# Attention step: Q projected directly behind K, z and output in the score banks, scores last; two qv_out buffers, one pos_qv

## What is computed

```
def step(carry, qkv):                      # two segments of 64 rows, one after the other
    mem, zc = carry
    qs, ks, vs = qkv
    sq = elu(qs) + 1.0
    mem = mem + einsum('bhsk,bhsv->bhkv', sq, vs)
    zc = zc + (elu(ks) + 1.0).sum(axis=-2, keepdims=True)
    scores = einsum('bhsk,bhtk->bhst', qs, ks) * scale
    att_dot = einsum('bhst,bhtv->bhsv', softmax(scores, axis=-1), vs)
    num = einsum('bhsk,bhkv->bhsv', sq, mem)
    den = sq.sum(axis=-1, keepdims=True) * zc
    att = gate * (num / den) + (1.0 - gate) * att_dot
    return ((mem, zc), att.reshape(Bx, L, H * DV) @ Wo)
x = layernorm(x + attention(x))
```

## Time and profile before

| | |
|---|---|
| timed runs, median (lowest to highest) | 1029.44 us (1025.58 to 1029.86) |
| profiled execution, its own time | 1023.68 us |
| its span | 1021.9 us |
| granted TensorE clock, mean over the span | 0.851 |
| PE busy | 791.6 us, 77% |
| DVE, ACT, POOL busy | 619.2, 542.7, 515.4 us |

### The profile page before, as it was taken

The page is one execution under the profiler, slowest core; times in us unless marked ns, Lnnn a source line. Parts: engine busy times, 40 slices in busy tenths (PEclk is TensorE's granted clock), DMA queues, the critical chain, the costliest instruction groups (busy, mean ns, idle before and its releaser), DMA issues. The chain is left out here.

```text
span 1021.9 us, 26750 instructions
## 1 busy us (share of the span) xinstructions
PE 791.6 (77%) x9501; PEld 683.3 (67%) x9502; DVE 619.2 (61%) x1217; ACT 542.7 (53%) x1119; POOL 515.4 (50%) x524
## 2 busy tenths in 40 slices
PE   5688898899988899889989899987599450099940
PEld 4577777787877778778778787877366450089940
DVE  4466666666766767666676676766588450034438
ACT  4656666656676566665676666672222110067730
POOL 2364546655565555565555645564334116546742
PEclk8788989988998989898898988998799655589985
DMA  6565655655655665565655656654118501140023
GB/s 211 133 179 137 146 135 144 144 165 144 144 144 144 165 150 138 144 144 165 156 132 144 149 161 149 138 146 123 49 32 232 64 1 44 52 107 31 31 74 111
DMA packets 115499, 127.71 MB, mean 125 GB/s; under 512 B 6913, under 2 KB 101409, under 8 KB 109329
## 3 DMA queue, kind: packets, MB, share of 16 engines
q1 hardware_dynamic: 112928, 122.17, 48.1%
q0 software_dynamic: 2544, 5.21, 1.5%
HBM read 67.42 MB, written 43.16 MB: 108 GB/s over the span
## 5 line engine op out<-in xcount | busy, mean ns | idle before, releaser
L304 POOL TENSOR_TENSOR ps<-s_exp,row_rec 128x512 f32<-128x512 f32 x64 | 66.7, 1045 | 202.5 <-DVE row_rec L669 202.5
L326 POOL TENSOR_TENSOR lhs<-pos_qv,ungate 64x1024 f32<-64x1024 f32 x64 | 150.6, 2353 | 2.5
L313 POOL TENSOR_TENSOR e_qk<-e_qk 128x512 f32<-128x512 f32 (+2 forms) x96 | 79.3, 826 | 90.0 <-DVE e_qk L637 85.0
L502 ACT ACTIVATE s_exp<-s_exp 128x512 f32<-128x512 f32 x64 | 40.2, 628 | 137.0 <-DVE s_exp L717 137.0
L645 DVE SCALAR_TENSOR_TENSOR qv_out<-bank,e_qk 128x512 f32<-128x512 f32 x64 | 44.2, 692 | 104.4 <-ACT e_qk L526 103.5
L401 PE MATMUL bank<-const,ps 128*128 128x128 f32 x512 | 94.1, 342 | 2.9 <-issue 2.5
L657 DVE TENSOR_TENSOR lhs<-mix,zg_all 64x512 f32<-64x512 f32 x128 | 88.3, 690 | 7.5 <-DMA zg_all<-scratch_z 3.6
L579 ACT ACTIVATE psT<-bank 128x512 f32<-128x512 f32 x128 | 72.4, 595 | 22.1 <-PE bank L401 21.8
L427 PE MATMUL bank<-kT,qkT 64*64 64x64 f32 x2048 | 83.0, 249 | 0.0
L372 PE MATMUL bank<-w_v,x_cur 128*128 128x512 f32 x192 | 77.7, 559 | 3.6 <-DVE w_v L603 3.6
L401 PEld LDWEIGHTS bank<-const,ps 128*128 128x128 f32 x512 | 74.3, 175 | 8.7 <-issue 3.0
(11 more groups left out here) (210 smaller groups left out, 1684.8 us busy)
## 6 DMA issues: line engine op xcount, KB each, us to landing
scratch_qv<-qv_out SPq DMA_DIRECT2D x32, 1024.0 KB, 4.0
pos_qv<-scratch_qv SPq DMA_DIRECT2D x64, 512.0 KB, 6.2
kT<-qkT SPq DMA_DIRECT2D x32, 512.0 KB, 4.1
zg_all<-scratch_z SPq DMA_DIRECT2D x64, 256.0 KB, 3.8
sorted_x<-padding SPq DMA_DIRECT2D x1, 2515.5 KB, 20.7
r_all<-in_x_dram SPq DMA_DIRECT2D x4, 512.0 KB, 6.7
cx<-in_ctx_dram SPq DMA_DIRECT2D x8, 256.0 KB, 2.8
w<-in_L_ffn_W_dram SPq DMA_DIRECT2D x1, 2048.0 KB, 9.4
```

The lines of the kernel that those rows point to most:

```text
L313: pool.tensor_tensor(dst, e_qk[:, 0:c, DK:], e_qk[:, c:2 * c, DK:], ALU.add).then_inc(k_summed, 1)
L326: pool.tensor_tensor(lhs[0:L, 1 - n, :, :], pos_qv[q][s, :, DK:], ungate[s, :, :], ALU.mult).then_inc(vg_ready, 1)
```

## The change

It writes the lists of the engines in another order and moves buffers:

- PE: Q is projected directly behind V and K. The z sum goes into score_bank[0] and the output into score_bank[1], where they were in proj_bank. output follows remember and is now for t - 2, no longer t - 3. All four turn_ps follow output, and the scores stand last in the step, where they were between the second and third turn_ps; they wait for res_ready, since the output shares their bank.
- qv_out has two buffers, pos_qv one. So SP's reload of pos_qv waits for mem_ready and vg_ready of the step before.
- DVE: sq_sum and its reciprocal stand directly behind zg and ahead of cut_k; evac_memory(0) stands ahead of cut_q(0), evac_memory(1) ahead of cut_q(1); the residual follows cut_q(1); all evac_memory precede the row maxima.
- ACT: the first exponential is at the head of the next step, evac_att behind the copies of Q, all four psT copies together.
- POOL: ps<-pos_qv stands ahead of k_sum, and the copy to x_cur last.

```diff
@@ attention_phase
-        qv_out = sb("qv_out", [P, C, 2 * DK])
+        qv_out = [sb(f"qv_out{i}", [P, C, 2 * DK]) for i in range(2)]
-        pos_qv = [sb(f"pos_qv{i}", [P, H, 2 * DK]) for i in range(2)]
+        pos_qv = sb("pos_qv", [P, H, 2 * DK])
@@ SP step
                     sp.wait_ge(stored_qv, 16 * t)
+                    if not is_step(u, 0):
+                        sp.wait_ge(mem_ready, 2 * u)
+                        sp.wait_ge(vg_ready, 2 * u)
@@ PE turn_qk
-                        pe.wait_ge(shifted, 2 * t - 1 + f)
+                        pe.wait_ge(*((z_rec, t), (shifted, 2 * t))[f])
@@ PE step
                     pe.wait_ge(v_evac, t + 1)
+                    for hh in range(2):
+                        project(proj_bank, w_q, hh, q_proj)
                 if two:
...
+                    pe.wait_ge(shifted, 2 * t - 1)
                     pe.wait_ge(k_summed, 4 * t)
-                    pe.matmul(proj_bank[0][0:SEG * H, 0:DK], cst("z_sum"), k_sum[:, :], start=True, stop=True).then_inc(zc_ready, 1)
-                if four:
...
-                    output(t - 3)
+                    pe.matmul(score_bank[0][0:SEG * H, 0:DK], cst("z_sum"), k_sum[:, :], start=True, stop=True).then_inc(zc_ready, 1)
                 if three:
                     attend(t - 2, 0)
                     attend(t - 2, 1)
                 if one:
-                    if is_step(t, 0):
-                        pe.wait_ge(w_split, 6)
-                    if two:
-                        pe.wait_ge(z_rec, t)
-                    project(proj_bank, w_q, 0, q_proj)
-                    if four:
-                        pe.wait_ge(res_ready, t - 2)
-                    project(proj_bank, w_q, 1, q_proj)
                     for f in range(4):
                         turn_qk(f)
                 if two:
                     remember(0)
                     remember(1)
-                    turn_ps(0)
-                    turn_ps(1)
-                if one:
+                if three:
...
+                    output(t - 2)
+                if two:
+                    for f in range(4):
+                        turn_ps(f)
+                if one:
+                    if three:
+                        pe.wait_ge(res_ready, t - 1)
                     score(0)
                     score(1)
-                if two:
-                    turn_ps(2)
-                    turn_ps(3)
@@ DVE step
                     dve.tensor_tensor(zg[:, :], z[:, :], gate[:, :], ALU.mult).then_inc(z_ready, 1)
+                if two:
+
+                    dve.wait_ge(qv_loaded, 32 * t)
+                    if not is_step(u, 0):
+                        dve.wait_ge(sqn_ready, u)
+                    dve.tensor_reduce(sq_sum[:, :], pos_qv[:, :, 0:DK], X, ALU.add).then_inc(sq_summed, 1)
+                    dve.wait_ge(sq_summed, t)
+                    dve.reciprocal(sq_rec[:, :], sq_sum[:, :]).then_inc(sq_inv, 1)
                 if one:
                     cut_k(0)
-                if not is_step(t, 0, 1, 2):
-                    residual(t - 3)
-                if one:
                     cut_k(1)
                 if not is_step(t, 0, 1):
                     move_att(t - 2)
                 if two:
-
-                    dve.wait_ge(qv_loaded[q], 32 * (hq + 1))
...
+                    evac_memory(0)
                 if one:
                     cut_q(0)
                 if two:
-                    evac_memory(0)
+                    evac_memory(1)
                 if one:
                     cut_q(1)
-                if two:
-                    evac_memory(1)
+                if not is_step(t, 0, 1):
+                    residual(t - 2)
+                if two:
+                    evac_memory(2)
+                    evac_memory(3)
```

More of the change, by code:

```diff
@@ L211, in attention_phase @@
         stored_qv, stored_z, z_loaded = sem("stored_qv"), sem("stored_z"), sem("z_loaded")
-        qv_loaded = [sem(f"qv_loaded{i}") for i in range(2)]
+        qv_loaded = sem("qv_loaded")
         vg_ready = sem("vg_ready")
@@ L358, in output @@
                 for c in range(C // 2):
-                    last = pe.matmul(proj_bank[1][:, 0:D], attT[:, c, :], w_o[:, c, :], start=(c == 0), stop=(c == C // 2 - 1))
+                    last = pe.matmul(score_bank[1][:, 0:D], attT[:, c, :], w_o[:, c, :], start=(c == 0), stop=(c == C // 2 - 1))
                 last.then_inc(out_ready, 1)
@@ L413, in remember @@
                         odd, at = h % 2, (h // 2 % 4 * 2 + n) * DK
-                        last = pe.matmul(mix[odd * DK:(odd + 1) * DK, h // 8, at:at + DK], pos_qv[q][0:k, h, 0:DK],
-                                         pos_qv[q][0:k, h, DK:], start=True, stop=True)
+                        last = pe.matmul(mix[odd * DK:(odd + 1) * DK, h // 8, at:at + DK], pos_qv[0:k, h, 0:DK],
+                                         pos_qv[0:k, h, DK:], start=True, stop=True)
                     last.then_inc(mem_ready, 1)
@@ L531, in step @@
                         act.wait_ge(v_proj, 2 * t + hh + 1)
-                        if hh == 0 and not is_step(t, 0):
-                            act.wait_ge(stored_qv, 16 * t)
-                        last = act.activation(qv_out[:, c, DK:], src, ACT.Copy)
+                        if hh == 0 and not is_step(t, 0, 1):
+                            act.wait_ge(stored_qv, 16 * u)
+                        last = act.activation(qv_out[p][:, c, DK:], src, ACT.Copy)
                     last.then_inc(v_evac, 1)
@@ L561, in step @@
                         act.activation(qk_tok[:, c, 0:DK], src, ACT.Copy).then_inc(q_evac, 1)
+                if three:
+                    evac_att(t - 2)
+                if one:
                     for f in range(4):
@@ L642, in cut_q @@
                     dve.wait_ge(q_grown, 2 * t + hh + 1)
-                    if hh == 0 and not is_step(t, 0):
-                        dve.wait_ge(stored_qv, 16 * t)
-                    dve.scalar_tensor_tensor(qv_out[:, c, 0:DK], proj_bank[hh][:, :].rearrange("p (c k) -> p c k", c=8), 0.0,
+                    dve.scalar_tensor_tensor(qv_out[p][:, c, 0:DK], proj_bank[hh][:, :].rearrange("p (c k) -> p c k", c=8), 0.0,
                                              e_qk[:, c, 0:DK], ALU.max, ALU.add).then_inc(sq_ready, 1)
@@ L692, in step @@
                 if two:
-                    dve.wait_ge(qv_loaded[q], 32 * (hq + 1))
-                    if not is_step(u, 0):
-                        dve.wait_ge(sqn_ready, u)
-                    dve.tensor_reduce(sq_sum[:, :], pos_qv[q][:, :, 0:DK], X, ALU.add).then_inc(sq_summed, 1)
-                    dve.wait_ge(sq_summed, t)
-                    dve.reciprocal(sq_rec[:, :], sq_sum[:, :]).then_inc(sq_inv, 1)
+                    evac_memory(0)
                 if one:
@@ L718, in step @@
                                           ALU.subtract).then_inc(shifted, 1)
-                if two:
-                    evac_memory(2)
-                    evac_memory(3)
             run_steps(dve, step, B, peeled=2)
-            residual(B - 2)
             move_att(B - 1)
```

56 lines of the change are left out of this document (23 added, 33 removed).

## The result

The changed kernel takes 1071.63 us (median of 4 runs, 1070.77 to 1072.03), the kernel before 1027.51 us beside it; the ratio is 1.043, 95% interval 1.040 to 1.046. The forecast was 1074 us, the range 1038 to 1108. The profiled execution of the changed kernel had 1071.37 us and a span of 1069.5 us.

What follows compares the result with a forecast made beforehand. A loop through the pos_qv store and reload was taken to bound each step: 21.9 us, with 0.9 for half clock 22.8. 1023.7 + 48.4 - 1.5 = 1070.6, and 3.4 more gives 1074 us, range 1038 to 1108.

Steps and rivals of the forecast that it cites:

- The loop: Reload landing through sq_sum, cut_k, move_att, remember, evac_memory and cut_q to store and next reload: 21.9 us a step, no slack.
- The toll of the clock: Half clock on TensorE's remember, behind idle time: 0.9 us a step taken, between bounds of nothing and 2.15.
- The upper bound: Half clock meeting remember in each step, taking twice as long: 2.15 us a step.
- The kT wait: TensorE's wait for kT ahead of the scores goes: 62.4 us in 32 times, 1.82 us in the step shown.
- The single pos_qv does not bind: The reload's wait for the single buffer: lhs ends at landing + 11.4 us, the reload is issued at + 13.9.
- The drain: End of the attention phase: saves about 1.5 us, as one output of 2.0 us is gone from it.
- Profiled against timed: Timed runs lie 1.9 to 6.2 us above the profiled execution, median 5.8; 3.4 us added.
- A loop without any toll: Rival: the loop through the reload at 21.9 us a step with no half-clock cost, 1046 us; chance 0.2.
- remember at half clock in every step: Rival: remember on TensorE always at half clock, 24.05 us a step, 1113 us; chance 0.16.
- "Faster": Rival: loop shorter than counted, TensorE still bounds, 19.4 us a step, 970 us; chance 0.05 with what lies between.
- The rule on waits: Issue a DMA early, wait late: by it sq_sum's new place is a loss, VectorE standing still about 2 us.

Runs made afterwards that it cites:

- e7: The changed kernel with qv_out stored twice, first into a row of scratch_qv that nobody reads: 1164.79 us, ratio 1.135.
- e3: The changed kernel with both cut_q ahead of the first two evac_memory, sq_sum still early: 995.43 us, ratio 0.973.
- e2: The changed kernel with sq_sum and its reciprocal behind cut_k and move_att, and x_cur's copy at the head of POOL's list: 1011.79 us, ratio 0.988.
- e6: The changed kernel with each group of attend matmuls issued twice in a row: 1058.85 us, ratio 1.032.
- e11: The changed kernel with two buffers for pos_qv again, nothing else: 1068.51 us, ratio 1.043.
- e10: The changed kernel with both cut_q ahead of evac_memory and two buffers for pos_qv: 967.49 us, ratio 0.944.
- e5: The kernel before with sq_sum and its reciprocal directly behind zg, ahead of cut_k: 1056.53 us, ratio 1.028.
- e1: The changed kernel with sq_sum and its reciprocal put back behind cut_k and move_att: 1053.18 us, ratio 1.028.
- e4: The changed kernel with sq_sum behind move_att, x_cur first on POOL and cut_q ahead of evac_memory: 982.95 us, ratio 0.959.
- e9: The changed kernel with cut_q ahead of evac_memory and x_cur's copy at the head of POOL's list, sq_sum still early: 997.37 us, ratio 0.974.
- e8: The changed kernel with sq_sum behind move_att, x_cur first, cut_q ahead of evac_memory and two buffers for pos_qv: 932.20 us, ratio 0.910.

## Why the prediction was right

- **The loop.** Counted 21.9 us at full clock, measured 21.87 in the step shown and 21.7 on average of the ten at full clock, and all of its links are in the timeline in the order given. e7 shows that there is no slack in it, e3 that it breaks when cut_q leaves it, e2 that it breaks when sq_sum does and x_cur does not take its place. The parts were off a little and balance: landing to cut_q 9.5 us measured from sq_sum (9.6 counted), store and reload to sq_sum 12.4 (12.3 counted).
- **The toll of the clock.** 0.9 us a step taken, 22.67 - 21.87 = 0.80 measured, 1.0 on remember's own busy time. It was put on the right instruction, but the number was a choice between two bounds, and that it fits is in part luck. The upper bound was too high: half clock costs remember 3.88 - 2.23 = 1.65 us and not 2.15 (the rows that I leaned on, 3.68 against 2.08, give a factor of 1.8 and not 2). And two thirds of the steps pay 1.45 each (23.2 against 21.7), the others nothing, which nothing in the prediction could have told. The cause I gave, idle time ahead of remember, was tested by e6 and holds for about 0.5 of the 0.8, with the idle time ahead of the transposes.
- **The kT wait** went, as forecast (6.3 us left).
- **The single pos_qv does not bind**: right for this kernel (e11, 3 us), but the loop of 19.6 us that I passed over as slack bound as soon as cut_q was early (e10).
- **The drain.** This step of the sum failed: forecast -1.5 us, measured +3.2. I counted the output that falls away and not that TensorE, idle for 7.1 us there, would run remember, the output and the first transposes at half clock.
- **Profiled against timed.** I added 3.4 us for the difference of the two; the changed kernel's profiled execution is 0.3 under its median. That the total came within 2.4 us is in part luck: the steps (48.4 forecast, 44.1 measured) and this offset were too high by 4.3 and 3.1, the drain too low by 4.7, and the start of the phase, 0.9 longer, was not in the sum.
- **The rivals.** A loop without any toll (21.9 a step) and remember at half clock in every step (24.05) are both out at 22.67 as a rule for all steps, though the first describes a third of them, and the second, at 23.2 and not 24.05, two thirds. "Faster" was right in its condition: it decides when the chain from cut_q to the landing no longer holds TensorE. e3 did it by starting the chain earlier, not by shortening it, and came out 2.7% below the kernel before.
- **The rule on waits.** The rule of the Trainium skill, DMA: Bandwidth & Descriptors, section Rules for kernel authors, to wait late, spoke against sq_sum's early place. The runs agree: that move alone made the kernel before 31 us slower (e5), and taking it back gave 18 us (e1), with x_cur early 60 (e2), and 14 once cut_q stood first (e4 against e9). It is not the whole of it: with the wait left early, storing sooner gave 76 us (e3).

## What to carry to other kernels

- In a software pipeline with a round trip through memory, follow the landing of the load through every in-order list back to the instruction that issues the next store. That sum is the least a step can take, whatever the busiest engine does. Here it was 21.9 us while TensorE had 18 us of work.
- What feeds the store goes ahead of what waits for the load. Two cut_q placed ahead of two evac_memory gave 76 us, where a later wait alone gave 18.
- When a loop is broken, the next one is close: e1 ran into x_cur, e3 into lhs and the single buffer. Work out the sums of the second and third loop before the edit, and expect one cure alone to show little or much depending on the others (3 us in e11, 28 us in e10, 51 us from e4 to e8).

## What the runs showed of the hardware

- More work made the kernel faster: with 60 us of repeated matmuls in idle places e6 took 13 us less, its clock 0.96 for 0.89 from 60 to 600 us.
- The granted clock of the attention steps went from 0.90 to 0.97 in e8 and to 0.99 in e10 from 60 to 600 us, with no change in the work. In e10 TensorE is busy 91% of that stretch (window of e10 below), before 89% at 0.90. The two shares are not of the same thing: at half clock the same matmuls count as busy for longer (17.12 and 20.23 us in the two steps of the earlier trace rows). The order of the work differs too, and no run isolates what the clock follows.

```profile
60.00:600.00 540.00, 490.51 (x7286) 421.76 (x7286) 384.02 (x671) 381.35 (x728) 329.78 (x279) 0.99 0.66 164
```

- A granted clock of 0.89 over many steps is a mean of two kinds of step. In the changed kernel remember, behind the same 0.80 us of idle time, takes 2.23 us in one step and 3.88 in the next.
- One store more in the queue, 1 MB, cost 2.7 us a step on the path in e7, while a store of 1 MB alone takes 4.0 us from issue to landing. The two are issued 0.6 us apart and overlap: the reload is issued 6.8 us behind the first of them on average, where it was 4.1 behind the single one.
